# First tiles' remainders moved from slots 2 and 3 to 28 and 29, the others six slots apart, `wo` conversions one slot later

## The reference

```
ctx   = causal_ema(x, tau_ctx)
wg    = sigmoid([x, ctx] @ Wg.T + bg);  gated = x * wg
h1    = gelu(x @ Wn1.T + bn1);          mod = 0.5 + sigmoid(h1 @ Wn2.T + bn2)
traces[d] = causal_ema(gated * mod[d], tau[d]);   temporal = sum_d traces[d] * softmax(blend)[d]
gate  = sigmoid(temporal @ Wtemp.T + btemp);      soma = gelu(x @ Wsoma.T + bsoma)
x     = x + layernorm((soma * gate) @ Wout.T) * gamma + beta
```

```
s_i   = relu(x @ share_wi[i]) @ share_wo[i]                 (i = 0, 1, 2)
e     = wa * relu(x @ wi[type]) @ wo[type] + wb * relu(x @ wi[type+1]) @ wo[type+1]
g     = softmax(relu([e, s_0, s_1, s_2][token 0] @ gate_w1) @ gate_w2)
x     = x + e*g_0 + s_0*g_1 + s_1*g_2 + s_2*g_3
```

## Time and profile before

| what | value |
|---|---|
| median of 3 runs | 1095.56 us (1095.53 to 1095.74) |
| the profiled execution | 1094.21 us, its span 1092.3 us |
| TensorE busy | 1074.0 us, 98% of the span |
| VectorE busy | 764.0 us, 70% |
| ScalarE busy | 398.9 us, 37% |
| mean granted TensorE clock | 0.998 of full speed |

### The profile page before, as it was taken

How to read it: one execution, slowest core, us unless ns; L and a number is a source line. 1 busy time by engine, 2 the same in 40 slices (tenths; PEclk the granted TensorE clock), 3 DMA queues, 4 the chain that set the end, 5 groups by cost and what they waited for, 6 DMA issues and landing times.

```text
span 1092.3 us, 12453 instructions
## 1 busy us (share of the span) xinstructions
PE 1074.0 (98%) x4754; PEld 862.7 (79%) x4754; DVE 764.0 (70%) x1245; ACT 398.9 (37%) x628; POOL 8.9 (1%) x20
## 2 busy tenths in 40 slices
PE   7899999999999999999999999999999999999998
PEld 5488777788887888878887888878888788888886
DVE  7979987499654995469753896549955598544234
ACT  6454445422334234332344223433234323322221
POOL 0000000000000000000000000000000000000000
PEclk9999999999999999999999999999999999999999
DMA  6359888676444564546544564545645465446550
GB/s 220 109 206 380 304 331 305 235 292 239 155 161 166 209 240 151 191 149 256 176 155 156 208 248 160 193 155 193 235 152 192 155 245 198 147 164 218 185 193 19
DMA packets 36476, 219.58 MB, mean 201 GB/s; under 512 B 4354, under 2 KB 4610, under 8 KB 14786
## 3 DMA queue, kind: packets, MB, share of 16 engines
q1 hardware_dynamic: 34114, 206.22, 52.4%
q0 software_dynamic: 2304, 12.58, 3.0%
HBM read 185.10 MB, written 33.69 MB: 200 GB/s over the span
## 4 chain that ended last, share of the span: by engine, by line
PE 87%; DVE 10%; issue 1%; ACT 1%; DMA 1%; SPq 0%; DVEq 0%
PE ps_up L581 13%; PE ps_up L582 13%; PE ps_up L583 13%; PE ps_down L582 12%; PE ps_down L583 12%; PE ps_down L581 12%; PE ps_aux L581 3%; PE ps_aux L583 3%; PE ps_aux L582 3%; DVE trace L1160 1%; DVE hid_lo L1063 1%; DVE trace L1191 1%; DVE wi L1055 1%; PE ps_aux L709 1%; DVE temporal L1200 1%
## 5 line engine op out<-in xcount | busy, mean ns | idle before, releaser
L1063 DVE SCALAR_TENSOR_TENSOR hid_lo<-ps_up,hid_hi 128x512 fp32r<-128x512 f32 x320 | 218.4, 685 | 272.5 <-ACT hid_hi L861 270.8
L861 ACT ACTIVATE hid_hi<-ps_up 128x512 fp32r<-128x512 f32 x320 | 191.2, 597 | 552.3 <-PE ps_up L583 551.7
L581 PE MATMUL ps_up<-x_hi_all,wi 128*128 128x512 f32 (+1 forms) x644 | 256.2, 398 | 0.1
L583 PE MATMUL ps_up<-x_hi_all,wi 128*128 128x512 f32 (+1 forms) x644 | 253.8, 394 | 0.0
L582 PE MATMUL ps_up<-x_lo_all,wi 128*128 128x512 f32 (+1 forms) x644 | 253.2, 393 | 0.0
L581 PE MATMUL ps_down<-hid_hi,wo 128*128 128x512 f32 x640 | 250.8, 392 | 1.4 <-DVE hid_lo L1063 1.0
L583 PE MATMUL ps_down<-hid_hi,wo 128*128 128x512 f32 x640 | 251.7, 393 | 0.0
L582 PE MATMUL ps_down<-hid_lo,wo 128*128 128x512 f32 x640 | 251.7, 393 | 0.0
L581 PEld LDWEIGHTS ps_down<-hid_hi,wo 128*128 128x128 f32 x640 | 120.2, 188 | 30.9 <-issue 2.6
L583 PEld LDWEIGHTS ps_up<-x_hi_all,wi 128*128 128x128 f32 x644 | 120.9, 188 | 29.1
L581 PEld LDWEIGHTS ps_up<-x_hi_all,wi 128*128 128x128 f32 x644 | 121.7, 189 | 27.6 <-DVE x_lo_all L1055 0.3
(11 more groups left out here) (202 smaller groups left out, 837.4 us busy)
## 6 DMA issues: line engine op xcount, KB each, us to landing
wi<-split_wi SPq DMA_DIRECT2D x70, 1024.0 KB, 4.8
wo<-split_wo SPq DMA_DIRECT2D x70, 1024.0 KB, 4.9
modb<-mod_scratch SPq DMA_DIRECT2D x28, 512.0 KB, 4.4
split_wi<-wi SPq DMA_DIRECT2D x10, 1024.0 KB, 6.6
split_wo<-wo SPq DMA_DIRECT2D x10, 1024.0 KB, 8.7
xt<-in_x SPq DMA_DIRECT2D x8, 512.0 KB, 6.3
split_wi<-ex POOLq DMA_DIRECT2D x4, 1024.0 KB, 7.9
split_wo<-ex POOLq DMA_DIRECT2D x4, 1024.0 KB, 6.6
```

Of the source, the lines that this page charges most:

```text
L581: pe.matmul(ps, w_hi, x_hi, start=start, stop=False)
L583: return pe.matmul(ps, w_lo, x_hi, start=False, stop=stop)
L861: act.activation(hid_hi[:, k % NU, :], ps_up[k % NU][:, :], ACT.Relu).then_inc(hid_hi_ready, 1)
L1063: dve.scalar_tensor_tensor(hid_lo[:, k % NU, :], ps_up[k % NU][:, :], 0.0, f32(hid_hi[:, k % NU, :]), ALU.max, ALU.subtract).then_inc(hid_ ...
```

## The change

The slots of the tiles' roundings (2 to 7) and remainders (0 to 7) are others, and in batch 0 `wo_round` and `wo_rest` of the same units come one slot later in ScalarE's and VectorE's queues.

```diff
-TILE_ROUNDS = {20: 2, 21: 3, 31: 4, 32: 5, 42: 6, 43: 7}
-TILE_RESTS = {2: 0, 3: 1, 26: 2, 27: 3, 33: 4, 34: 5, 44: 6, 45: 7}
+TILE_ROUNDS = {33: 2, 34: 3, 39: 4, 40: 5, 45: 6, 46: 7}
+TILE_RESTS = {28: 0, 29: 1, 34: 2, 35: 3, 40: 4, 41: 5, 46: 6, 47: 7}
...
-                if b == 0 and k % 4 == 0 and m + 1 < UNITS:
+                if b == 0 and k % 4 == 1 and m + 1 < UNITS:
                     wo_round(m + 1)
...
-                if b == 0 and k % 4 == 1 and (k + 3) // 4 < UNITS:
-                    wo_rest((k + 3) // 4)
+                if b == 0 and k % 4 == 2 and k // 4 + 1 < UNITS:
+                    wo_rest(k // 4 + 1)
```

## The result

| | before | changed |
|---|---|---|
| median of 4 runs | 1095.55 us | 1105.53 us (1104.73 to 1106.05) |
| profiled execution, its span | 1094.21, 1092.3 us | 1104.73, 1102.2 us |

The ratio is 1.0094, with an interval of 1.0078 to 1.011: 10.0 us slower. The forecast was 4.6 us slower, with a range that ended at 1102.8. The sign was right, the size was not.

The account below looks back on a forecast made before the run. The prediction took the chain of waits to run through TensorE for 87% of the span and VectorE for 10%. Terms 0.75 + 2.7 + 1.13 = 4.6 us gave 1098.8 profiled, 1100.2 on the median, range 1097.0 to 1102.8.

Parts of the forecast that it names:

- Parts 1 and 2: Batch 0, slots 2 to 27: removed remainders' gain goes into waits for ScalarE; slot 20 about 0.5 us later, slot 27 +0.07.
- Part 3, term 1: Slots 28 to 34: `out` 0.38 us earlier, but `wo_rest(8)` delays the statistics, so `turn` starts later: +0.75 us.
- Part 4, term 2: Slots 34 to 41: tile 5's late landing holds ScalarE's rounding and Gelu, so `soma` waits: +2.7 us, bounds 1.2 and 4.8.
- the third pair: Before's third store and load pair of tiles: 14.5 us from second store's issue to second load's landing; 14.8 forecast for tile 5.
- a rival of 0.08: TensorE's clock falls to half behind the wait before `soma`, costing 1.7 us more: +6.3 us, 1101.9; chance 0.08.
- Part 5, term 3: Batch 1: VectorE late by one more tile remainder, shown at `hid_lo(61)` to `hid_lo(65)` and `tgate`: +1.13 us, bounds 0.9 and 1.2.

Follow-up runs that it names:

- Experiment 2: Kernel before with only the two new tables of the tiles' rounding and remainder slots, `wo` conversions as before: 1.0047, median 1100.08 us against 1094.47.
- Experiment 1: Changed kernel with both tile tables as before, so only the later `wo` conversions: 1.0019, 1096.33 us against 1094.47.
- experiment 10: Changed kernel with SP's load of weight unit 1 of batch 1 issued behind the load of slot 40: 1.0105 against before, 1106.42 us.
- Experiments 3: Changed kernel with tiles 4 and 5 rounded in slots 42 and 43, 6 and 7 in 49 and 50, remainders one slot later: 1.0020, 1096.72 us.
- 8: Changed kernel measured once more, on one chip with its filled version: 1.0091 against before, 1104.82 us against 1094.87.
- 9: Changed kernel with 22 products into an unused bank before `soma` of batch 1, rerun on the changed kernel's chip: 1.0073 against before, 1102.0 us.
- Experiment 5: Changed kernel with `modb2` issued behind the weight load of the same slot in SP's queue: 1.0082 against before, 1103.85 us against 1094.89.
- Experiments 6: Changed kernel, tiles 4 and 5 rounded in slots 42 and 43, 6 and 7 in 49 and 50, EMA_FIRST 3.5 not 4.5: 1.0020, 1096.94 us.
- best_b: Kernel before with tile remainders 0, 1, 3 in slots 0, 1, 28, gate part in slot 32, EMA_FIRST 3.5: 0.9986, 1093.38 us against 1094.89.

## Why the prediction was wrong

**Parts 1 and 2: right.** Waits of 0.81 and 0.71 us stand before `hid_lo(6)` and `hid_lo(8)`, slot 20 is 0.39 later (0.5 forecast) and waits for `wo_rest(5)`, slot 27 is at +0.04 (+0.07). Experiment 2 shows the core of it by itself: two remainders removed, 0.0 gained by slot 25.

**Part 3, term 1: right.** +0.67 at slot 34 against +0.75, with `out` at -0.48 against -0.38. Experiment 1 adds that the same lateness goes through `read_out` when a rounding stands there, which I had not named.

**Part 4, term 2: the step that failed.** The mechanism was right in each link: load, rounding, table load, Gelu, bank, `soma`. Its size was +2.7, and it was 7.1. Of this, the transfer is 2.2: the wait from the end of the product before was to be 2.7 and was 4.9 (5.15 from start to start less a step of 0.23). From the issue of the second store (189.8) to the landing of tile 5 (206.6) it took 16.8 us, not 14.8. I had taken a value near the third pair, when I had just said that SP's queue would be busy from the start. In the seven profiled executions with both parts of the change, and SP's loads beside the tiles as they were, this pair took 16.7 to 18.9 us, and with the tiles alone (experiment 2) 15.8. The slowest pair of before, 16.9, was the nearer case: SP's weights, stores and `modb` ran beside it all the time. That company sets the time is what experiment 10 shows; which of SP's transfers made the 2 us was not isolated. The wait of 4.9 was just past the term's upper bound (4.8), and the clock had no place in the term or its bounds.

The other 2.2 are the clock. I had this as a rival of 0.08 with a price of 1.7. The records show the clock at half for 6.8 us, 4.5 of which TensorE worked, hence 2.2 lost. The two belong together: the price of a wait of TensorE was to be reckoned with the clock behind it, not as a case of its own. Experiments 3, 8 and 9 show both: without the wait slot 42 is at +0.65, and with the wait filled it costs 2.1 less.

The Trainium skill ("TensorE: Matmul & The Clock Gate", section "HAM oscillation — how this bites in real kernels") speaks of just this, an engine that waits for a DMA (here by way of ScalarE's queue) and starts its next products cold. The trace agrees, with 0.42 us from product to product behind the wait (210.34 to 210.76) instead of 0.23. I had the sentence and gave it too little weight, because the only fall in the trace of before came in the sparse opening.

The Trainium skill ("ScalarE: Activation LUTs", section "What ACT_TABLE_LOAD costs"), which I weighed in part 4, gives a drain beside the load. The changed kernel has a load at 207.71 and the Gelu at 209.00, 1.29 later, with work queued directly ahead and behind: no drain of that size here either.

**Part 5, term 3: the size nearly, the place wrong.** Forecast 1.13 through `hid_lo` and `ct_lo`, measured +1.5 net: 1.74 in slot 54, and 0.25 less at slot 66. VectorE's lateness of one remainder is there. But `modb2` in SP's queue waits for VectorE, the weight load of the next unit stands behind it (0.4 us later than `modb2`, at 247.95) and then takes 8.6 instead of 6.6 us beside the last store of the tiles. TensorE's pause there gave VectorE its time back, so that `hid_lo` never stopped it. I had looked at SP's queue for the tiles, but not for who waits behind `modb2`. Experiment 5 takes the weight load ahead and finds the size, 1.14, but only 0.69 of it in the place that I had given (`hid_lo` and `tgate`); the first 0.45 wait for the next weight load, in slot 58.

**The range.** Its ends don't follow from the bounds: the forecast of 1100.2 with 1.2 and 4.8 in place of 2.7 gives 1098.7 and 1102.3, not 1098.5 and 1102.4. That changes nothing here.

**What stays open.** Why this execution's opening was 0.6 us longer. The slots add up to 9.3, and the medians differ by 10.0 at first and 9.95 the second time, when the profiled execution had 9.56 in the slots and 1.11 in the opening. Of the first four executions the two with the longest spans (1103.7 and 1104.1 us, against 1102.2 profiled) had the lowest mean clock, 0.995 against 0.997. That fits a longer wait with more time at half speed, but they have no trace. Experiments 6 and best_b ended elsewhere than expected, and their reason is read from the slots, not tested.

## What to carry to other kernels

Work that is taken out of an engine's queue gains only up to the next wait for somebody who is on time. Look for that wait first. A rounding or copy that waits for a DMA belongs behind whatever a bottleneck needs from the same queue, not ahead of it. And price a transfer by an earlier one that had the same company on the DMA engines, and a wait of TensorE of some microseconds with the slow clock behind it.

## What the runs showed of the hardware

TensorE's granted clock fell to half behind single waits in otherwise busy stretches. With the wait of 2.60 us (experiment 2) it was at half for 3.4 us, with 4.75 (the changed kernel) for 6.8, with 8.32 (experiment 10) for 10.2. With `turn`'s 1.73 us it stayed full. Products into an unused bank kept it full where the changed kernel waits 4.83 us (experiments 8 and 9). In the opening, with waits of 1.2 us between few products, it fell once in the kernel before and not at all in the changed one. Loads of 0.5 MB for the tiles took 3.8 to 13.2 us from issue to landing. The 13.2 are of experiment 1's kernel, where the load was issued 0.7 us behind a store of 1 MB in its own queue. What SP's queue moved at the time counted too: with one of its loads moved away from tile 4's and beside tile 5's, the first took 4.1 instead of 8.6 us and the second 10.9 instead of 5.4 (experiment 10).
